# Products over 192 features as a pass of 128 rows and a pass of 64, with the 64-row passes of two products side by side

## What is computed

```python
for l in range(2):
    q, k, v = (x @ W.T + b for W, b in (Wq, Wk, Wv))       # products over 192 features
    a = softmax(band(q @ k.T / 4), global key 0) @ v        # per head, window of 128, 4 query tiles
    x = ln(x + a @ Wo.T + bo)                                # over 192 features
    x = ln(x + relu(x @ W1.T + b1) @ W2.T + b2)              # W1 over 192 features, W2 over 768
```

## Time and profile before

| | us |
|---|---|
| median of 3 runs | 2574.18 (2573.77 to 2579.31) |
| profiled execution, its own time | 2564.87 |
| its span, first to last instruction | 2563.0 |
| TensorE busy in the span | 2097.3 (82%) |
| VectorE, ScalarE, GpSimd busy | 1300.9, 1125.2, 756.2 |
| the tower's 16 items, first score product to last | 79.2 to 1284.3 |
| one item of 24 steps (item 8, 679.80 to 756.87) | 77.07, TensorE busy 73.58 |

### The profile page before, as it was taken

How to read it: one execution, slowest core, us unless ns; L and a number is a source line. 1 busy time by engine, 2 the same in 40 slices (tenths; PEclk the granted TensorE clock), 3 DMA queues, 4 the chain that set the end, 5 groups by cost and what they waited for, 6 DMA issues and landing times. The chain is left out here.

```text
span 2563.0 us, 44046 instructions
## 1 busy us (share of the span) xinstructions
PE 2097.3 (82%) x14745; PEld 1487.9 (58%) x14745; DVE 1300.9 (51%) x4329; ACT 1125.2 (44%) x2396; POOL 756.2 (30%) x950
## 2 busy tenths in 40 slices
PE   5799999999999999999953567778776449999944
PEld 4466666666666666666642345545544239999931
DVE  2466555666555666555623345565444313333358
ACT  2466666665665666665610233333332113333322
POOL 0021212221212221212221012243444525555543
PEclk7799999999999999999975678776766569999965
DMA  3732233342234332233002322223121176777632
GB/s 99 123 66 49 38 41 63 63 63 46 37 45 85 63 63 44 35 50 63 2 2 76 70 51 50 61 69 72 44 52 40 55 247 209 235 230 225 188 98 90
DMA packets 119393, 211.48 MB, mean 83 GB/s; under 512 B 23236, under 2 KB 52038, under 8 KB 118520
## 3 DMA queue, kind: packets, MB, share of 16 engines
q1 hardware_dynamic: 108024, 189.29, 32.5%
q0 software_dynamic: 10176, 17.09, 2.1%
q10 hardware_dynamic: 976, 2.30, 0.3%
HBM read 149.82 MB, written 66.82 MB: 85 GB/s over the span
## 5 line engine op out<-in xcount | busy, mean ns | idle before, releaser
L675 ACT ACTIVATE tower_prob<-tower_prob,tower_negmax 128x386 f32<-128x386 f32 (+1 forms) x768 | 390.4, 556 | 303.2 <-DVE tower_negmax L882 302.5
L882 DVE CUSTOM_DVE_ANT_0 tower_prob<-tower_sbank,tower_band 128x386 f32<-128x386 f32 (+1 forms) x768 | 346.4, 489 | 142.4 <-PE tower_sbank L449 137.1
L487 PEld LDWEIGHTS tower_tbank<-tower_ident,tower_prob 128*128 128x128 f32 x1920 | 227.8, 143 | 129.5 <-issue 81.7
L487 PE MATMUL tower_tbank<-tower_ident,tower_prob 128*128 128x128 f32 x1920 | 284.4, 279 | 22.0 <-DVE tower_probT L907 20.4
L731 ACT ACTIVATE tower_probT<-tower_tbank 128x384 f32<-128x384 f32 (+1 forms) x576 | 227.6, 430 | 127.4 <-PE tower_tbank L487 124.8
L2000 POOL DMA_INDIRECT scratch_yt<-experts_y,experts_rows x190 | 185.8, 978 | 204.1 <-DVE experts_y L2151 171.7
L426 PE MATMUL tower_dbank<-tower_oxT,tower_w 96*128 96x512 f32 x384 | 191.4, 624 | 14.9 <-ACT tower_oxT L720 14.9
L2059 PE MATMUL experts_ybank<-experts_w,experts_hid 128*128 128x128 f32 x1520 | 186.8, 277 | 0.0
L2047 PE MATMUL experts_hbank<-experts_zT,experts_w 128*128 128x256 f32 x760 | 184.2, 386 | 1.0 <-issue 1.0
L449 PE MATMUL tower_sbank<-tower_k_st,tower_q_st 49*128 49x386 f32 (+1 forms) x768 | 161.1, 414 | 26.0 <-POOL tower_k_st L631 14.6
L2059 PEld LDWEIGHTS experts_ybank<-experts_w,experts_hid 128*128 128x128 f32 x1520 | 178.9, 193 | 0.1
(11 more groups left out here) (318 smaller groups left out, 3453.4 us busy)
## 6 DMA issues: line engine op xcount, KB each, us to landing
experts_w<-ew SPq DMA_DIRECT2D x95, 578.0 KB, 3.9
scratch_qk<-tower_qk SPq DMA_DIRECT2D x64, 384.0 KB, 4.8
tower_q_st<-scratch_qk SPq DMA_DIRECT2D x96, 192.0 KB, 7.9
tower_k_st<-scratch_qk SPq DMA_DIRECT2D x96, 192.0 KB, 10.9
experts_rows<-scratch_zs SPq DMA_DIRECT2D x95, 132.0 KB
scratch_kq<-induce_kq SPq DMA_DIRECT2D x8, 1024.0 KB, 4.3
experts_res<-scratch_yt SPq DMA_DIRECT2D x8, 1024.0 KB, 5.5
induce_k_st<-scratch_kq SPq DMA_DIRECT2D x48, 128.0 KB, 4.2
```

What stands on the lines that cost most here:

```text
L487: mm = pe.transpose(bank[:, jb * P:jb * P + P], prob[:, hg % PR, at + jb * P:at + jb * P + P], ident[:, :])
L675: act.activation(prob[:, hg % PR, 0:width(i)], prob[:, hg % PR, 0:width(i)], ACT.Exp, bias=negmax[:, hg % PR:hg % PR + 1], scale=-1.0).the ...
L882: scores.copied(dve.tensor_tensor_reduce(prob[:, hg % PR, 0:width(i)], bank[:, 0:width(i)], band[:, BAND_AT[i]:BAND_AT[i] + width(i)], sca ...
```

## The change

The 192 features are laid out as 128 partitions and 64. The 64-feature part of each transposed sequence is written twice, on partitions 0 to 63 and on 64 to 127, and so are the weights for it (or two products' different weights on the two halves). A product is then a matmul of 128 rows and one of 64, and the 64-row matmuls of two products are issued one behind the other on the two row halves, into two banks.

- `turn`: transposes of 128 and of 64 columns. ScalarE copies the first with one activation and the second with two (`parts`), for xT, oT and x1T.
- q and k: at p=1 and 3 `first_half` claims two banks and runs the 128-row matmuls of two products. At the start of the next step, ahead of the scores, `halves` runs their two 64-row matmuls. ScalarE and VectorE copy the four products out at p=2, 3, 4, 5 instead of 1 to 4.
- hidden layer: the same at p=13, 15, 17, the 64-row matmuls at 14, 16, 18, where both blocks are copied out.
- v at p=9 alone and the output projection at p=8 alone: `by_rows` claims two banks, runs four matmuls of 128 rows, then two side-by-side pairs of 64 rows. The product for the global key's value moves from p=11 to 10.
- a fifth parameter tensor, `gain`, is loaded per layer.

```diff
-        A_XT, A_QK, A_QG, A_SG, A_V, A_PGT, A_OG, B_OG1 = 0, (1, 2, 3, 4), 5, 6, (9, 10), 12, 23, 1
-        C_OT, C_O, C_STAT, C_X1, C_UP, C_DOWN = 5, (7, 8), 9, 12, range(13, 19), range(19, 23)
+        A_XT, A_QK, A_QK_OUT, A_QG, A_SG, A_V, A_V0, A_PGT, A_OG, B_OG1 = 0, (1, 3), (2, 3, 4, 5), 5, 6, 9, 10, 12, 23, 1
+        C_OT, C_O, C_STAT, C_X1, C_UP, C_DOWN = 5, 8, 9, 12, (13, 15, 17), range(19, 23)
+            def by_rows(keys, lhs, rhs):
+                banks = [dense.claim(pe, key) for key in keys]
+                for t in range(NT):
+                    pe.matmul(banks[t // 2][:, t % 2 * D:t % 2 * D + D], lhs[:, 0, t * P:t * P + P], rhs[:, 0:D],
+                              start=(t % 2 == 0), stop=False, skip_group_check=True)
+                for j in range(2):
+                    for e, bank in enumerate(banks):
+                        t, half = 2 * e + j, slice(HALF * e, HALF * e + HALF)
+                        mm = pe.matmul(bank[:, j * D:j * D + D], lhs[half, 1, t * P:t * P + P], rhs[half, D:2 * D],
+                                       start=False, stop=(j == 1), skip_group_check=True)
+                        if j:
+                            dense.filled(mm, keys[e])
+            def first_half(keys, lhs, rhs, rows_):
+                banks = [dense.claim(pe, key) for key in keys]
+                for bank, w in zip(banks, lhs):
+                    pe.matmul(bank[0:rows_, :], w, rhs, start=True, stop=False)
+                return banks
+            def second_half(keys, banks, lhs, rhs, rows_):
+                for e, (key, bank) in enumerate(zip(keys, banks)):
+                    half = slice(HALF * e, HALF * e + HALF)
+                    dense.filled(pe.matmul(bank[0:rows_, :], lhs[half, :], rhs[half, 1, :], start=False, stop=True),
+                                 key)
+            def halves(g):
+                n, p = divmod(g, PAIRS)
+                if is_item(n + 1) and p - 1 in A_QK:
+                    m, w = n + 1, A_QK.index(p - 1)
+                    keys = [("qk", m, w, c) for c in range(2)]
+                    second_half(keys, open_.pop(keys[0]), wqk[m // B][:, w, D:D + DP], xT, DP)
+                if is_item(n - 1) and p - 1 in C_UP:
+                    m, j = n - 1, C_UP.index(p - 1)
+                    keys = [("up", m, c) for c in (2 * j, 2 * j + 1)]
+                    second_half(keys, open_.pop(keys[0]), w1[:, FF + j * P:FF + j * P + P], oxT, P)
...
             for g in STEPS:
                 n, p = divmod(g, PAIRS)
+                halves(g)
                 if has_pair(g):
...
+            def parts(k):
+                return (slice(0, P),) if k == 0 else (slice(0, HALF), slice(HALF, P))
...
-                            dense.copied(act.activation(xT[:, k, :], bank[0:DP, :], ACT.Copy), ("xT", m, k))
-                    if p in A_QK:
-                        w, c = divmod(A_QK.index(p), KT)
+                            for part in parts(k):
+                                ins = act.activation(xT[part, k, :], bank[0:part.stop - part.start, :], ACT.Copy)
+                            dense.copied(ins, ("xT", m, k))
+                    if p in A_QK_OUT:
+                        w, c = divmod(A_QK_OUT.index(p), KT)
...
-                    if p in C_UP and C_UP.index(p) % 2 == 0:
-                        relu(m, C_UP.index(p))
+                    if p - 1 in C_UP:
+                        relu(m, 2 * C_UP.index(p - 1))
...
-                if p in A_V:
-                    t = A_V.index(p)
+                for t in range(2) if p == A_V else ():
                     bank = dense.take(dve, ("v", m, t))
```

More of the change, by code:

```diff
@@ L338, in turn @@
                 for t in range(NT):
-                    mm = pe.transpose(bank[0:DP, t * P:t * P + P], src[:, t, k * DP:k * DP + DP], ident[:, :])
+                    if k == 0:
+                        mm = pe.transpose(bank[:, t * P:t * P + P], src[:, t, 0:P], ident[:, :])
+                    else:
+                        mm = pe.transpose(bank[0:HALF, t * P:t * P + P], src[:, t, P:D], ident[:, :])
                 dense.filled(mm, key)
[L342 to L348, removed]
+            def by_rows(keys, lhs, rhs):
[10 more added lines that the diff above has]
+                            dense.filled(mm, keys[e])
@@ L362, in before @@
                             dense.wait_copied(pe, ("xT", m, k))
[L363 to L367, removed]
+                    keys = [("qk", m, w, c) for c in range(2)]
+                    open_[keys[0]] = first_half(
+                        keys, [wqk[layer][:, w, c * DP:c * DP + DP] for c in range(2)], xT[:, 0, :], DP)
                 if p == A_SG:
@@ L378, in before @@
                     dense.filled(mm, ("sg", m))
-                if p in A_V:
-                    t = A_V.index(p)
-                    by_rows(("v", m, t), xT, wvo[layer][:, 0, :, :], (2 * t, 2 * t + 1), KT)
-                if p == A_V[1] + 1:
+                if p == A_V:
+                    by_rows([("v", m, t) for t in range(2)], xT, wvo[layer][:, 0, :])
+                if p == A_V0:
                     dense.wait_copied(pe, ("v", m, 0))
@@ L408, in after @@
                         turn(("oT", m, k), x, k)
[L409 removed]
+                if p == C_O:
                     for k in range(KT):
                         dense.wait_copied(pe, ("oT", m, k))
[L412 to L413 removed]
+                    by_rows([("o", m, t) for t in range(2)], oxT, wvo[layer][:, 1, :])
                 if p == C_X1:
@@ L423, in after @@
                             dense.wait_copied(pe, ("x1T", m, k))
[L424 to L428, removed]
+                    cs = (2 * j, 2 * j + 1)
+                    open_["up", m, 2 * j] = first_half([("up", m, c) for c in cs],
+                                                       [w1[:, c * P:c * P + P] for c in cs], oxT[:, 0, :], P)
                 if p in C_DOWN:
@@ L433, in after @@
                             dense.wait_copied(pe, ("up", m, c))
-                    by_rows(("down", m, t), hid, w2, (t,), FC)
+                    bank = dense.claim(pe, ("down", m, t))
+                    for c in range(FC):
+                        mm = pe.matmul(bank[:, 0:D], hid[:, c, t * P:t * P + P], w2[:, c, :],
+                                       start=(c == 0), stop=(c == FC - 1))
+                    dense.filled(mm, ("down", m, t))
             for g in STEPS:
                 n, p = divmod(g, PAIRS)
+                halves(g)
                 if has_pair(g):
@@ L713, in _ @@
                                 dense.take(act, ("up", m - 1, FC - 1))
-                            dense.copied(act.activation(oxT[:, k, :], bank[0:DP, :], ACT.Copy), ("oT", m, k))
+                            for part in parts(k):
+                                ins = act.activation(oxT[part, k, :], bank[0:part.stop - part.start, :], ACT.Copy)
+                            dense.copied(ins, ("oT", m, k))
                     if p == C_X1:
@@ L719, in _ @@
                                 dense.take(act, ("o", m, 1))
-                            dense.copied(act.activation(oxT[:, k, :], bank[0:DP, :], ACT.Identity,
-                                                        scale=cols[m // B][:, 2, k:k + 1],
-                                                        bias=cols[m // B][:, 3, k:k + 1]), ("x1T", m, k))
-                    if p in C_UP and C_UP.index(p) % 2 == 0:
-                        relu(m, C_UP.index(p))
+                            for part in parts(k):
+                                ins = act.activation(oxT[part, k, :], bank[0:part.stop - part.start, :], ACT.Identity,
+                                                     scale=gain[m // B][part, 0, k:k + 1],
+                                                     bias=gain[m // B][part, 1, k:k + 1])
+                            dense.copied(ins, ("x1T", m, k))
+                    if p - 1 in C_UP:
+                        relu(m, 2 * C_UP.index(p - 1))
                 if has_pair(g - 1):
```

59 lines of the change are left out of this document (34 added, 25 removed).

## The result

The changed kernel takes 2819.39 us (median of 4 runs, 2809.78 to 2825.10), the kernel before 2573.97 in the same comparison. The ratio is 1.0952, 95% interval 1.0910 to 1.0995: slower by 245 us, where 2800 was forecast in a range of 2665 to 2890.

A forecast was written before the change was run, and what follows sets the result against it. TensorE's own work was taken to set most steps' time. Net added time of 11.0 us per item (162 us) and 68 us of falling clock on 2564.87 profiled gave 2795, plus 9.3 is 2804, rounded to 2800; range 2665 to 2890.

The forecast's parts named there:

- the clock: Behind TensorE's stops: two falls to half clock per item, 4.5 us taken between 0 and 9, 68 us in all.
- The work saved: TensorE's matmuls: 4.7 us per item for five pairs, 0.36 twice for the rows, 86 us in all if nothing waits.
- The rival of the other side: Evictions come before TensorE gets to the claims, so the saved work passes through: 2488 us; chance 0.07.
- The overlap: A pair's 64-row matmuls run side by side on the row halves, 0.85 us; one after the other, 1.71.
- The stop of step 3: TensorE idles 6.7 us ahead of the k products, whose second bank still holds the second q product.
- The rival without VectorE's lag: VectorE's queue order differs, so step 3 stops 3.5 us and not 6.7: 2672 us; chance 0.11.
- The stops of step 5: TensorE waits ahead of oT's two blocks: the first until 17.5 us, the second until 21.0, from step 2's start.
- TensorE's wait of 1.02 us at step 5: In the kernel before, a 1.0 us wait for VectorE's probability copy, put down to the normalisation (1.23 us) queued ahead.
- The layout: ScalarE's third activations: +0.54 us per item at step 1 for xT and +0.7 for x1T; oT's is hidden.
- The smaller waits: Waits outside steps 3 and 5: at hidden-layer steps 15, 17, 19 and in the rows' steps 7, 9 and 10.
- The hidden layer: Steps 14 to 19: waits for banks eat what the halves save and 0.5 us more per item.
- The rows: v and output projection: +0.4 us at step 7 for probability copies, +1.4 at steps 9 and 10, per item.

The follow-up runs named there:

- e7_fill: The changed kernel with idle matmuls added on TensorE in the stops at steps 3 and 5; 2746.37 us, ratio 1.0675 to the kernel before.
- e11_single: As e10_x1t, but no product paired and no early copies of q, k and hidden blocks; 2591.12 us, ratio 1.0011 to the kernel before.
- e10_x1t: As e9_alone, but VectorE copies the second block of x1T and ScalarE only the first; 2504.11 us, ratio 0.9688 to the kernel before.
- e8_early: The changed kernel with q, k, hidden copies ahead of exponentials, pair banks claimed singly, normalisation at step 5; 2555.93 us, ratio 0.9928 to before.
- e5_serial: The changed kernel with both 64-row matmuls of every pair on the lower row half; 2905.26 us, ratio 1.1282 to the kernel before.
- e6_norm: The changed kernel with the second layer norm's root and normalisation at steps 4 and 5, finish at 6; 2831.08 us, ratio 1.0990 to before.
- e1_layout: The changed kernel's layout and third activation, but every product alone at its old step; 2588.37 us, ratio 1.0071 to the kernel before.
- e3_up: As e1_layout, but the hidden layer's products paired as in the changed kernel; 2600.03 us, ratio 1.0104 to the kernel before.
- e4_rows: As e1_layout, but v and output projection paired as in the changed kernel; 2647.85 us, ratio 1.0295 to the kernel before.
- e9_alone: As e8_early, but v and output projection as before the change, normalisation at step 1; 2526.92 us, ratio 0.9759 to the kernel before.

## Why the prediction was right

**The sum.** An item grew by 16.3 us (77.09 to 93.35); the forecast was 11.0 and 4.5 for the clock. The tower grew by 235 us (1205.1 to 1439.7, first score product to last) where 162 + 68 = 230 was said; the part behind it, which no term covered, is 9 us longer, and it lies between 1279 and 1297 us in all thirteen kernels. The time, 2819, is 19 above the forecast. That the sum is so near is in part luck, since two terms err against each other. e7_fill, with the clock up in steps 3 to 8, grew by 11.5 us per item over before, 2.0 of it in step 12, where its clock falls. That leaves some 9.5 for the waits and exposed copies, where 11.0 was said, and 6.8 for the clock in the changed kernel, where 4.5 was said. The waits were taken too long in steps 1 to 5 (7.4 where 8.0 was said) and in steps 13 to 19 (0.5 where 1.2 was said).

**The work saved.** Shown, and of the forecast size: e11_single to e10_x1t, TensorE's busy time over eight items falls from 591.7 to 552.3, 4.9 us per item for five pairs where 4.7 was said. The rival of the other side (2488) was right about its price and not about its condition: the evictions do not come before the claims, and the stops are far over 5.4 us per item, as e8_early shows by taking them away.

**The overlap.** Shown by e5_serial: 0.85 us more of busy time per pair, and 4.3 us per item in the steps of the five pairs, as forecast. The totals, 86 us and 83 said, are closer than they deserve, as falls of the clock moved as well. The bound from the single-record scores and the double-record value products carried over to 64-row fp32 products.

**The stop of step 3.** 6.41 us, forecast 6.7; the chain is the one followed, event by event. The rival without VectorE's lag (3.5 us) fell: e6_norm took the normalisation out and the stop shrank by its length. **The stops of step 5.** 1.36 and 2.80 us against 1.6 and 3.1 (16.1 to 17.5 and 18.15 to 21.0 in the times followed, with 0.2 for the release).

**A reading of the kernel before that was wrong.** The forecast put TensorE's wait of 1.02 us at step 5 down to the normalisation. The normalisation stands in step 3; there it costs a wait of 0.36 us. With it at step 1, in e11_single, step 3 is 0.3 us shorter and the wait of step 5 is still 1.0. At step 5 VectorE's probability copy stands behind k's last remainder, which waits 1.35 us for ScalarE (below, VectorE in the kernel before). No term of the sum rested on it.

```profile
699.07 0.75 DVE L797 SCALAR_TENSOR_TENSOR tower_qk<-tower_dbank,tower_cols,tower_qk 96x512 fp32r<-96x512 f32 x1 [1.35 <-ACT tower_qk L698]
699.74 0.54 DVE L907 COPY tower_probT<-tower_tbank 128x384 f32<-128x384 f32 x1
```

**The layout.** 1.3 us per item in e1_layout for the two exposed activations (0.57 at step 1, 0.75 at steps 13 to 19), 1.24 said. A 64-row copy costs ScalarE what one of 128 rows costs (572 to 598 ns over both forms), so the upper end of that bound was the right one.

**The smaller waits.** The hidden layer: 0.3 us per item net in e3_up, 0.5 said. The rows: 3.5 in e4_rows; 1.8 was said for the waits of steps 7 to 10, and they grew by 1.7. The rest, 2.0, is in step 12, where the clock falls; the clock term of the forecast counted two falls and did not name this one.

**The clock.** The term was 4.5 us, taken between 0 and 9 as two short falls behind the stops. It was too small. e7_fill measured 5.8 for those two in the mean: 4.1 to 4.5 in the five items with the short second fall, as was said, and 8.4 to 8.6 in the three with the long one. The third fall comes on top; it was not priced by itself in the changed kernel, whose step 12 is 1.4 us longer than before. What the forecast had not seen is that the clock can undo a gain: in e6_norm a shorter stop bought nothing in the mean.

## What to carry to other kernels

Before two products are paired, follow the banks they hold: the claim that comes next must not need a bank whose reader stands in its queue behind work that waits for the claimer. Where such a ring has closed, move the copy to a point where its engine is idle: here that, with the order changes that go with it, turned a loss of 9.5% into a gain of 0.7% with all pairs kept, and of 3.1% once the pairs of v and the output projection were given up and x1T's second copy moved. And price a stop of TensorE at more than its length: what runs behind it may run at half clock, and shortening the stop a little need not pay (e6_norm). When work is moved to a later step, look also at the queues that wait for its result only once: one item of e8_early lost 15 us in that way.

## What was unexpected of the hardware

- Useless matmuls in a stop made the kernel faster: 7.7 us of them per item took 4.75 us off it (e7_fill).
- A wait of 1.35 us, among score products and transposes, was followed by half clock for the next steps in each item (e4_rows). One of 1.8 us at step 13 was not in items 4 to 11 of e1_layout, and was in half of them in e9_alone; one of 1.02 us at step 5 of the kernel before never was in its items 1 to 14.
- The fall behind one and the same stop lasts 6.8 us in some items and 17.1 in others, and an item takes 4.5 us more with the long one.
